# Quarter-array masks, halved values and router products, a merged shift, a re-sorted prologue and regenerated order lists in a two-layer gated model

## The chip, the cores and the metric

The kernel runs on one core of a Trainium2 chip. The metric is the device time of one execution in microseconds (us). Of the kernel before, three runs are shown.

## What is computed

Input x is 8 sequences of 256 tokens of 128 values. Two gated steps follow each other; each adds s * silu(g) to x.

```
xn = layernorm(x)
s  = scan of 32 states over time, y = (c * state) @ Wy + xn @ Wd + biases
g  = two layers of: token shift (upper 64 channels from the token before);
     8-head attention of width 64 in windows of 64 with look-back 64,
     q and k normalised, rotated and scaled; @ wo; residual;
     shift, layernorm, gated GELU MLP of 341; residual
x  = x + s * silu(g)
xn = layernorm(x)
s  = causal attention over 256 tokens, 16 heads of width 8
g  = mixture of 16 experts (SwiGLU 128-256-128, layernorm), two per token
x  = x + s * silu(g)
```

The local attention's mask: with i a query and j a key of its own or the previous window, `(i < j) | (i > j + 64) | (j == -1)` is masked.

## The kernel before, in words

The tokens are 16 tiles of 128 rows. Phase A handles four tiles (two sequences b = 0, 1) in each of four **turns**; phase B ("final") routes tokens and loads experts; phase C runs 48 expert tiles and the output. Phase A is cut into sections: HEAD (the first tiles' norm, q, k, v), FIRST (turn 0), BODY (a hardware loop over turns 1 and 2), TAIL (turn 3) and LAST (the rest of the small attention and the routing). FIRST and BODY also hold the beginning of the next turn; BODY, TAIL and LAST carry the small attention of the turn before (its items begin with b: bqk, bS, bE, bT, bP, bN, bO).

**The order of the work is a computed list.** `PARTS` gives each kind of item its engines and an assumed duration on each; `section_order` runs a list scheduler over them once, at build time, and writes one fixed list per engine. Each engine walks its own list in `run`, in order, and waits on semaphores. So a changed number in `PARTS` changes no arithmetic, and may reorder every engine.

Items that the text speaks of, all for layer l and sequence b: "x" transposes the normalised tiles; "qk" n is one product 128x512 of q or k, then ACT squares it, DVE sums the squares and multiplies by two tables (line 1457), POOL takes the power -0.5 (line 1800) and adds the rotated halves (line 1803), DVE scales (line 1465, item "scale"), PE transposes ("qkT", line 938). "S" is the pair of score banks of one 128-query tile (`scores`), "E" the exponential, "T" the transposes of the probabilities (line 821), "V" the product with the values (`values`), "O" the division, "oT", "wo", then "sh", the shift product, "nh" the layernorm, "hT", three "w1", "w2". "gate" forms the new x, "nm1" and "x1T" norm and transpose it, "router" makes its logits. "ab", "c", "scan", "y" are the state branch.

`scores` opens each of its two banks with one bf16 product, identity (128x128) times a 128x512 mask (line 801), and then adds 16 products of 64 rows by 64 columns each, in four positions of the array (line 812). `values` has, for the first query tile (qt = 0), one product per head with all 128 probability columns as stationary operand, and for qt = 1 two, each with 64 columns. f32 products appear as two records each in the trace, transposes and bf16 products as one.

The prologue: SP issues all loads (x whole, rope tables, first weights, small attention weights, 41 small loads, 2 more, then 12 zero fills of a scratch). POOL makes all constants (identities, shift matrices, masks; lines 1748 to 1775) before anything else. PE and ACT first transpose and copy the five small-attention weights (lines 877, 879), DVE first scales four rope tables (line 1374), and only then does the first tile's norm start (line 1409).

## Time and profile before

| | us |
|---|---|
| median of 3 runs | 936.89 |
| lowest, highest | 935.74, 938.36 |
| the profiled execution's own time | 931.56 |
| its span in the profile | 929.7 |
| PE busy | 727.6 (78%) |
| DVE busy | 635.4 (68%) |
| ACT busy | 506.0 (54%) |
| POOL busy | 391.5 (42%) |

PE is TensorE, DVE VectorE, ACT ScalarE, POOL GpSimd, SP SyncE, which only issues transfers. Times inside the trace count from the span's start. A row of a timeline gives start, length, engine, line, operation, tiles and shape; what stands in brackets is the idle time before it and what ended it. "xN" is a number of instructions. PEclk is the share of the full TensorE clock that was granted.

### The profile page before, as it was taken

The numbers are of one execution on the slowest core, as the hardware profiler recorded it, in microseconds if no ns is written. First come the engines' busy times: TensorE is split into PE (matmuls) and PEld (weight loads), VectorE is DVE, ScalarE is ACT, GpSimd is POOL, SyncE is SP. The second block draws the span as 40 slices with busy tenths as digits, with TensorE's granted clock in tenths as the row PEclk, the third lists the DMA queues.
The fourth block names the chain that finished last, engine by engine and source line by source line (L and its number), as shares of the span: only waits on it lengthen the run. The fifth ranks groups of instructions, "written<-read, shape, count | busy, mean of one in ns | idle before, by whom it ended". The sixth has DMA issues, their size and how long they took to land.

```text
span 929.7 us, 19949 instructions
## 1 busy us (share of the span) xinstructions
PE 727.6 (78%) x6997; PEld 547.7 (59%) x7031; DVE 635.4 (68%) x1521; ACT 506.0 (54%) x901; POOL 391.5 (42%) x470
## 2 busy tenths in 40 slices
PE   2589787599898875898988769885997689698840
PEld 1256465367676753576767447762775567598730
DVE  2586685588779664977796759638676499276645
ACT  1255455365766653756766446543656275487711
POOL 4560651670335034705340545009300437458880
PEclk9799998799999997999999979989999599899975
DMA  5700000000000000000000000000000345212104
GB/s 154 213 1 1 1 1 1 1 1 2 1 2 1 2 1 2 1 2 1 2 1 2 1 2 1 2 1 0 2 2 1 92 135 180 84 59 80 59 38 144
DMA packets 41963, 29.70 MB, mean 32 GB/s; under 512 B 7570, under 2 KB 39308, under 8 KB 41612
## 3 DMA queue, kind: packets, MB, share of 16 engines
q1 hardware_dynamic: 39308, 23.18, 8.6%
q0 software_dynamic: 2560, 5.25, 1.5%
q8 instruction: 60, 0.98, 0.4%
q14 instruction: 35, 0.29, 0.1%
HBM read 18.98 MB, written 9.44 MB: 31 GB/s over the span
## 4 chain that ended last, share of the span: by engine, by line
PE 44%; DVE 20%; POOL 12%; issue 12%; ACT 8%; DMA 1%; SPq 1%; DVEq 0%; POOLq 0%; ACTq 0%
PE psM L782 19%; PE psT L821 4%; ACT arena L1132 4%; PE psO L866 4%; PE psS L851 4%; DVE arena L1457 3%; PE psO L782 3%; PE psS L812 3%; DVE PR L1349 3%; POOL arena L1800 3%; POOL arena L1803 3%; POOL yt_scratch L1826 3%; ACT L1132 2%; POOL RS L1782 2%; DVE arena L1465 2%
## 5 line engine op out<-in xcount | busy, mean ns | idle before, releaser
L782 PE MATMUL psM<-arena 128*128 128x128 f32 (+7 forms) x1168 | 269.3, 374 | 48.0 <-DVE arena L1457 30.3
L1132 ACT ACTIVATE arena<-psT 128x512 f32<-128x512 f32 (+3 forms) x296 | 149.6, 530 | 128.6 <-PE psT L821 44.9
L782 PEld LDWEIGHTS psM<-arena 128*128 128x128 f32 (+5 forms) x1168 | 158.6, 193 | 102.0 <-DVE arena L1457 44.3
L1132 ACT ACTIVATE arena<-psM 128x512 f32<-128x512 f32 (+2 forms) x168 | 88.4, 542 | 126.6 <-PE psM L782 125.7
L1781 POOL TENSOR_SCALAR RS<-MV 128x2 f32<-128x2 f32 x56 | 12.9, 231 | 304.0 <-DVE MV L1490 211.6
L1343 DVE TENSOR_REDUCE MX<-psS 128x4 f32<-128x512 f32 (+1 forms) x160 | 102.7, 683 | 44.9 <-PE psS L851 22.9
L1800 POOL TENSOR_TENSOR arena<-arena,powm 128x8 f32<-128x8 f32 x64 | 109.5, 1711 | 5.3
L1132 ACT ACTIVATE PR<-PR 128x512 f32<-128x512 f32 x160 | 94.9, 626 | 21.0 <-DVE PR L1349 20.7
L1349 DVE TENSOR_TENSOR PR<-psS,MX 128x512 f32<-128x512 f32 x160 | 102.2, 680 | 0.0
L821 PE MATMUL psT<-ident,PR 128*128 128x128 f32 x640 | 91.4, 278 | 10.5 <-ACT PR L1132 6.8
L821 PEld LDWEIGHTS psT<-ident,PR 128*128 128x128 f32 x640 | 71.9, 143 | 34.3 <-issue 22.9
L1803 POOL TENSOR_TENSOR arena<-arena 128x512 f32<-128x512 f32 x64 | 84.1, 1313 | 0.0
L1457 DVE TENSOR_TENSOR arena<-psM,arena 128x512 f32<-128x512 f32 x128 | 81.8, 681 | 3.3 <-POOL arena L1803 3.3
L1132 ACT ACTIVATE arena<-arena 128x768 f32 (+3 forms) x61 | 46.5, 763 | 57.1 <-DVE arena L1722 30.2
L1132 ACT ACT_TABLE_LOAD x51 | 65.4, 1283 | 2.1 <-PEq L1904 1.2
L1799 POOL TENSOR_SCALAR arena<-arena 128x8 f32<-128x8 f32 x64 | 18.2, 284 | 109.9 <-DVE arena L1448 109.3
L1465 DVE TENSOR_TENSOR arena<-arena 128x512 f32<-128x512 f32 x64 | 49.9, 802 | 19.8 <-POOL arena L1803 19.8
L782 PEld LDWEIGHTS psO<-arena,PT 128*64 128x64 f32 (+1 forms) x768 | 48.2, 155 | 14.9 <-issue 11.3
L1448 DVE TENSOR_REDUCE arena<-arena 128x8 f32<-128x512 f32 x64 | 43.5, 679 | 19.5 <-ACT arena L1132 19.1
L851 PE MATMUL psS<-arena 32*128 32x256 f32 (+1 forms) x512 | 55.7, 346 | 0.0
L1826 POOL DMA_INDIRECT yt_scratch<-arena,DEST x48 | 49.9, 1040 | 12.2 <-issue 6.7
L782 PE MATMUL psO<-arena,PT 128*64 128x65 f32 (+1 forms) x768 | 51.5, 241 | 2.9 <-ACT PT L1132 2.9
(196 smaller groups left out, 1142.5 us busy)
## 6 DMA issues: line engine op xcount, KB each, us to landing
arena<-in_L_ffn_w SPq DMA_DIRECT2D x50, 128.0 KB, 2.4
xg_scratch<-zeros SPq DMA_DIRECT2D x12, 256.0 KB, 4.0
arena<-xg_scratch SPq DMA_DIRECT2D x12, 256.0 KB
arena<-yt_scratch SPq DMA_DIRECT2D x4, 512.0 KB, 5.3
arena<-in_L_ffn_wqkv SPq DMA_DIRECT2D x2, 768.0 KB, 5.0
arena<-in_L_ffn_ln_g SPq DMA_DIRECT2D x1, 1024.0 KB, 7.5
arena<-in_L_ffn_ln_b SPq DMA_DIRECT2D x1, 1024.0 KB, 10.4
out<-arena SPq DMA_DIRECT2D x4, 256.0 KB, 2.2
```

The source lines that it names most:

```text
L782: return nc.tensor.matmul(o, lhsT, rhs, start=start, stop=stop)
L821: last = nc.tensor.transpose(bank[:, c * P:(c + 1) * P], PR[:, m % 4, c * P:(c + 1) * P], ident[:])
L851: last = nc.tensor.matmul(Sb[i][:, c * keys:(c + 1) * keys], QL[r, b, lane, qt * P:(qt + 1) * P], KT1[r, b * SEQ:b * SEQ + keys], start=False,
L1132: return nc.scalar.activation(o, i, f, **kw)
L1343: V.tensor_reduce(maxima[i], scores[i], AX, ALU.max).then_inc(dstep, 1)
L1349: V.tensor_tensor(PR[:, (n + i) % 4, :].rearrange("p (s k) -> p s k", s=ns), scores[i], maxima[i].unsqueeze(2).broadcast_to([P, ns, 512 // ...
L1448: V.tensor_reduce(SS[:, m % 4, :], SQ[:, m % 2, :].rearrange("p (h d) -> p h d", h=8), AX, ALU.add).then_inc(ss_done.sem(m), 1)
L1457: last = V.tensor_tensor(dst.rearrange("p (h d) -> p h d", h=8), src, RT[:, 2 * l + n % 2, x, t % 2, :].unsqueeze(1) .broadcast_to([P, 8, ...
L1465: V.tensor_tensor(r1, r1, RN[:, m % 4, :].unsqueeze(2).broadcast_to([P, 8, DH]), ALU.mult)\
L1800: G.tensor_tensor(RN[:, m % 4, :], RN[:, m % 4, :], powm[:, 0:8], ALU.pow)
L1803: G.tensor_tensor(r1, r1, r2[:, :, ::-1, :], ALU.add).then_inc(rope_sum.sem(m), 1)
L1826: G.indirect_dma_start(YT, bass.IndirectOffsetOnAxis(DEST[:, tile:tile + 1], 0), YO[:, tile % OUT_RING, :], None)\
```

## The change

`PARTS`: S on PE 1.8 to 1.5, V 0.9 to 0.6, sh 0.7 to 0.5, router 1.5 to 0.6. All lists are computed anew from them. In `scores` the mask product of a bank becomes two products of 64 rows by 64 columns by 512, so that a pair of banks has four, one in each quarter of the array; two masks with their halves exchanged are made by four transfers from SBUF to SBUF. `values` uses two 64-column products for both query tiles. The shift product of two tiles becomes one of 128 columns. The router's four products become eight of 64 columns. In the prologue x's first four tiles and layer 0's weights come first, 14 loads of the state branch move to ACT's queue, POOL makes only one identity and `powm` first and the rest after the first rstd, layer 0's tables are scaled inside the first "qk", and the small-attention weights are turned after HEAD, through the two O banks.

```diff
-    "S": (("PE", 1.8), ("DVE", 2.4)), "E": (("ACT", 0.58),), "T": (("PE", 0.5), ("ACT", 0.6)),
-    "V": (("PE", 0.9),), "O": (("DVE", 0.7),),
+    "S": (("PE", 1.5), ("DVE", 2.4)), "E": (("ACT", 0.58),), "T": (("PE", 0.5), ("ACT", 0.6)),
+    "V": (("PE", 0.6),), "O": (("DVE", 0.7),),
...
@@ block.sync
-            sp.dma_start(XALL[:], ins["L0_attn_x"].rearrange("b (t p) d -> p (b t) d", p=P)).then_inc(ld_x, 16)
+            sp.dma_start(XALL[:, 0:GT], x_in[:, 0:GT]).then_inc(ld_x0, 16)
+            sp.dma_start(WQKV[:, 0].rearrange("p s n -> p (s n)"), ins["L0_ffn_wqkv"][0]).then_inc(ld_qkv, 16)
...
-            sp.wait_ge(dve_consts, 1)
+            sp.dma_start(XALL[:, GT:NT], x_in[:, GT:NT]).then_inc(ld_x, 16)
...
             sp.wait_ge(pool_consts, POOL_CONSTS)
+            for m, v in zip(swapped, (mask0[0], mask1)):
+                for h in range(2):
+                    sp.dma_start(m[64 * h:64 * h + 64], v[64 - 64 * h:P - 64 * h]).then_inc(ld_masks, 16)
...
@@ scores
                 for i in range(2):
                     pe.wait_ge(s_free.sem(n + i), s_free.reuse(hs, n + i))
-                    nc.tensor.matmul(Sb[i][:], identb[:], (mask0[0], mask1)[qt][:], start=True, stop=False,
-                                     skip_group_check=True)
+                    pe.sem_inc(pe_settled, 1)
+                    r = slice(64 * i, 64 * i + 64)
+                    for w in range(2):
+                        nc.tensor.matmul(Sb[i][64 * w:64 * w + 64, :], identb[r, r],
+                                         ((mask0[0], mask1)[qt] if w == i else swapped[qt])[r, :], start=True, stop=False,
+                                         skip_group_check=True)
@@ values
-                    if qt == 0:
-                        last = mm(bank[:, o], p, VA[:, 2 * b, head, :])
-                    else:
-                        mm(bank[0:64, o], p[:, 0:64], VC[:, b, head, :])
-                        last = mm(bank[64:P, o], p[:, 64:P], VA[:, 2 * b + 1, head, :])
+                    mm(bank[0:64, o], p[:, 0:64], VC[:, b, head, :] if qt else VA[:, 2 * b, head, :])
+                    last = mm(bank[64:P, o], p[:, 64:P], VA[:, 2 * b + qt, head, :])
@@ block.tensor, after HEAD
+            def after_head():
+                pe.wait_ge(ld_raw, 16 * 5)
+                for c in range(4):
+                    last = nc.tensor.transpose(Ob[0][:, c * P:(c + 1) * P], WRAW[:, c, :], ident[:])
+                last.then_inc(raw_turned, 1)
+                nc.tensor.transpose(Ob[1][:, 0:E], WRAW[0:E, 4, :], ident[0:E, 0:E]).then_inc(raw_turned, 1)
+                pe.wait_ge(ld_s5, LOADED_S5)
@@ "sh"
-                        mm(bank[:, 0:64], shift[:], XC[:, 2 * b, 64:D])
-                        mm(bank[:, 64:128], shift[:], XC[:, 2 * b + 1, 64:D], True, False)
-                        mm(bank[:, 64:128], carry[:], XC[:, 2 * b, 64:D], False, True).then_inc(m_full.sem(sec.M[item]), 1)
+                        nc.tensor.matmul(bank[:, 0:128].rearrange("p (t d) -> p t d", t=2), shift[:],
+                                         XC[:, 2 * b:2 * b + 2, 64:D], start=True, stop=False, skip_group_check=True)
+                        nc.tensor.matmul(bank[:, 64:128], carry[:], XC[:, 2 * b, 64:D], start=False, stop=True,
+                                         skip_group_check=True).then_inc(m_full.sem(sec.M[item]), 1)
@@ "router"
-                            last = mm(bank[:, t * E:(t + 1) * E], XN1T[:, t * P:(t + 1) * P], RWT[:])
+                            for h in range(2):
+                                tokens = slice(t * P + 64 * h, t * P + 64 * h + 64)
+                                last = mm(bank[64 * h:64 * h + 64, t * E:(t + 1) * E], XN1T[:, tokens], RWT[:])
@@ block.scalar
+            act.wait_ge(dve_consts, 1)
+            for dst, src in s5_loads:
+                act.dma_start(dst, src).then_inc(ld_s5, 16)
...
             def after_head():
+                act.wait_ge(raw_turned, 2)
+                for i, w in enumerate((WQT, WKT, WVT, WOT)):
+                    act_fn(w[:], Ob[0][:, i * P:(i + 1) * P], ACT.Copy)
+                act_fn(RWT[:], Ob[1][:, 0:E], ACT.Copy).then_inc(raw_kept, 1)
@@ block.vector, first "qk" of HEAD
+                        if sec is HEAD and n == 0:
+                            dve.wait_ge(ld_first, LOADED_FIRST)
+                            scaled_tables(0).then_inc(tables, 1)
+                            dve.wait_ge(tables, 1)
@@ block.gpsimd
+                        if sec is HEAD:
+                            constants()
```

The waits for late loads move to their first use in FIRST: `ld_masks` and `pool_consts` before "S", `raw_kept` before "V", `ld_a` before "wo" and "hT".

**Where instructions move.** First ACT at the very start of the program. Before:

```order
0 L1129 UNCONDITIONAL_BRANCH
1 L1132 ACT_TABLE_LOAD
2 L1132 ACTIVATE WQT<-psT 128x128
3 L1132 ACTIVATE WKT<-psT 128x128
4 L1132 ACTIVATE WVT<-psT 128x128
5 L1132 ACTIVATE WOT<-psT 128x128
6 L1132 ACTIVATE RWT<-psT 128x16
7 L1132 ACTIVATE arena<-psT 128x256
```

And with the change:

```order
7 L1177 DMA arena<-in_L_attn_Wd 128x128
8 L1177 DMA arena<-in_L_attn_Wy 32x128 x2
9 L1177 DMA arena<-in_L_attn_by 128x128
10 L1177 DMA arena<-in_L_attn_bd 128x128
11 L1160 ACT_TABLE_LOAD
12 L1160 ACTIVATE arena<-psT 128x256
13 L1160 ACTIVATE arena<-psT 64x256
```

The 14 transfers now stand ahead of ACT's table load and of its copies for "x"; the five weight copies have moved behind HEAD.

Second, PE in TAIL (the fourth turn), where layer 1's "qk" and "qkT" (line 938, now 955) of the first sequence are issued. L845 (now 857) with L851 (863) is "bS", L821 (836) is "T" or "bT", psM 128x512 is "qk" or "v", L902 (917) is "x". Before:

```order
502 L902 MATMUL psT<-ident,arena 128x128 x2
503 L782 MATMUL psM<-arena 128x512 x3
504 L938 MATMUL psT<-ident,arena 128x128 x4
505 L782 MATMUL psM<-arena 128x512
506 L938 MATMUL psT<-ident,arena 128x128 x4
507 L782 MATMUL psM<-arena 128x512
508 L938 MATMUL psT<-ident,arena 128x128 x4
509 L782 MATMUL psM<-arena 128x512
510 L938 MATMUL psT<-ident,arena 128x128 x4
511 L782 MATMUL psM<-arena 128x512
```

With the change:

```order
545 L917 MATMUL psT<-ident,arena 128x128 x2
546 L793 MATMUL psM<-arena 128x512
547 L836 MATMUL psT<-ident,PR 128x128 x4
548 L793 MATMUL psM<-arena 128x512
549 L955 MATMUL psT<-ident,arena 128x128 x4
550 L857 MATMUL psS<-maskc,identb 128x512 x2
551 L863 MATMUL psS<-arena 128x128 x8
552 L793 MATMUL psM<-arena 128x512
553 L836 MATMUL psT<-ident,PR 128x128 x12
554 L793 MATMUL psM<-arena 128x512 x2
555 L955 MATMUL psT<-ident,arena 128x128 x8
556 L857 MATMUL psS<-maskc,identb 128x2x128 x2
```

Before, nothing of the small attention's second sequence stood among these; now "bqk" of it, three of its six "bS" and six of its twelve "bT" stand ahead of layer 1's "S". In BODY the same happens more mildly. There PE had, in layer 1, the first "S" and at once the "x" of the second sequence:

```order
282 L801 MATMUL psS<-maskl,identb 128x512 x2
283 L812 MATMUL psS<-arena 64x128 x16
284 L899 REGISTER_ALU
285 L902 MATMUL psT<-ident,arena 128x128 x2
286 L782 MATMUL psM<-WOT,arena 128x128 x2
```

and has now:

```order
314 L827 MATMUL psS<-arena 64x128 x16
315 L793 MATMUL psM<-arena 128x128 x6
316 L836 MATMUL psT<-ident,PR 128x128 x4
317 L799 REGISTER_ALU
318 L836 MATMUL psT<-ident,PR 128x128 x4
319 L804 REGISTER_ALU
320 L793 MATMUL psM<-WVT,arena 128x128 x2
321 L793 MATMUL psO<-arena,PT 64x65 x8
322 L833 REGISTER_ALU
323 L836 MATMUL psT<-ident,PR 128x128 x4
324 L857 MATMUL psS<-maskc,identb 128x2x128 x2
325 L863 MATMUL psS<-arena 128x256 x4
```

with the "x" of the second sequence only behind these rows (both "S" of the first sequence stand ahead of them). Of BODY's 172 PE items 107 keep their relative order; HEAD's and LAST's lists are unchanged.

## Rows read from the trace of the kernel before

**Rows 1.** Stretches; busy PE, PEld, DVE, ACT, POOL (instructions), clock, DMA share, GB/s
```profile
0.00:38.30 38.30, 14.62 (x35) 5.96 (x35) 15.66 (x37) 10.09 (x21) 22.92 (x44) 0.98 0.69 188
38.30:185.00 146.70, 112.66 (x908) 79.15 (x914) 98.15 (x228) 70.87 (x126) 60.82 (x66) 0.92 0.04 10
...
367.10:546.60 179.50, 153.68 (x1560) 113.08 (x1568) 133.80 (x288) 107.83 (x186) 67.48 (x74) 0.97 0.01 2
546.60:724.00 177.40, 149.05 (x1529) 111.93 (x1536) 121.39 (x267) 100.34 (x171) 53.45 (x60) 0.94 0.01 1
...
804.00:929.70 125.70, 77.42 (x628) 73.53 (x628) 72.72 (x263) 65.55 (x125) 73.12 (x96) 0.84 0.24 76
```

**Rows 2.** Timeline of the prologue: start us, length us, engine, line, tiles
```profile
1.20 1.28 ACT L1132 ACT_TABLE_LOAD   x1 [1.20 <-PEq L1904]
...
1.85 0.27 DVE L1366 MEMSET arena<- 128x256 f32 x1 [1.85 <-issue]
...
9.26 0.41 POOL L1775 TENSOR_SCALAR_AFFINE_SELECT maskl<-maskl 64x256 bf16<-64x256 bf16 x1
...
10.16 0.42 SPq L734 DMA_DIRECT2D arena<-in_L_attn_Wa  x1
...
11.71 1.43 DVE L1374 TENSOR_TENSOR arena<-arena 128x256 f32<-128x256 f32 x4 [9.24 <-DMA arena<-in_L_ffn_k_scale]
...
13.18 0.49 DVE L1409 BATCH_NORM_STATS2 ST<-XALL 128x6 f32<-128x128 f32 x2
...
16.95 1.03 ACT L1132 ACTIVATE arena<-psT 128x256 f32<-128x256 f32 x3 [2.21 <-PE psT L902]
...
18.03 3.78 PE L782 MATMUL psM<-arena 128*128 128x512 f32 x4 [1.19 <-ACT arena L1132]
...
21.66 0.25 POOL L1799 TENSOR_SCALAR arena<-arena 128x8 f32<-128x8 f32 x1 [6.37 <-DVE arena L1448]
...
30.49 9.96 SPq L740 DMA_DIRECT2D xg_scratch<-zeros  x12
...
34.38 1.26 POOL L1803 TENSOR_TENSOR arena<-arena 128x512 f32<-128x512 f32 x1
```

**Rows 3.** DMA issues of the first 14 us: KB each, us to landing
```profile
XALL<-in_L_attn_x SPq DMA_DIRECT2D x1, 0.5 KB, 6.6
```

**Rows 4.** Timeline of PE: masks, values, router beside what follows each
```profile
274.01 0.59 PE L801 MATMUL psS<-maskl,identb 128*128 128x512 bf16 x2
274.53 1.10 PE L812 MATMUL psS<-arena 64*64 64x128 f32 x32
...
282.88 1.90 PE L782 MATMUL psO<-arena,PT 128*128 128x65 f32 x16
284.61 1.08 PE L782 MATMUL psM<-arena 128*128 128x512 f32 x2
...
387.36 0.69 PE L782 MATMUL psO<-arena,PT 128*64 128x65 f32 x16
387.97 0.66 PE L961 MATMUL psT<-ident,arena 128*128 128x128 f32 x4
...
544.47 1.89 PE L782 MATMUL psM<-RWT,arena 128*128 128x16 f32 x8 [0.55 <-ACT arena L1132]
```

**Rows 5.** Groups of PE by shape, whole run: busy us, mean ns, idle before
```profile
L782 PE MATMUL psM<-arena,shift 128*128 128x64 f32 x64 | 9.5, 271 | 0.0
```

**Rows 6.** Chain of waits, fourth turn: shares by line
```profile
by line: PE psM L782 23.6%; issue 7.9%; PE psT L821 7.1%; PE psO L866 6.3%; PE psS L851 6.1%; PE psO L782 5.9%; POOL arena L1800 5.9%; POOL arena L1803 5.2%; DVE PR L1349 4.1%; PE psS L812 4.0%; ACT arena L1132 3.9%; PE psT L961 2.3%; ACT L
```

**Rows 7.** Two stretches of the fourth turn, columns as in rows 1
```profile
631.00:655.00 24.00, 15.28 (x79) 7.88 (x80) 17.24 (x28) 10.84 (x20) 22.97 (x21) 0.93 0.00 0
655.00:715.00 60.00, 54.61 (x673) 44.11 (x675) 42.48 (x101) 40.99 (x67) 6.87 (x12) 1.00 0.01 2
```

**Rows 8.** The page, groups of DVE: busy us, mean ns, idle before
```profile
L1343 DVE TENSOR_REDUCE MX<-psS 128x4 f32<-128x512 f32 (+1 forms) x160 | 102.7, 683 | 44.9 <-PE psS L851 22.9
...
L1349 DVE TENSOR_TENSOR PR<-psS,MX 128x512 f32<-128x512 f32 x160 | 102.2, 680 | 0.0
```

More of the change, by code:

```diff
@@ L106 @@
     "gate": (("ACT", 0.42), ("DVE", 1.9), ("Pool", 1.0)), "nm1": (("DVE", 0.6),),
-    "x1T": (("PE", 0.3), ("ACT", 0.4), ("Pool", 0.4)), "router": (("PE", 1.5), ("DVE", 0.3)),
+    "x1T": (("PE", 0.3), ("ACT", 0.4), ("Pool", 0.4)), "router": (("PE", 0.6), ("DVE", 0.3)),
     "bqk": (("PE", 1.9), ("ACT", 0.75)), "bqm": (("Pool", 0.95),), "bv": (("PE", 0.5), ("DVE", 0.42)),
@@ L474, in gated_layers @@
         mask1 = sb("maskl1", [P, 512], BF16)
+        swapped = [sb(f"swapped{k}", [P, 512], BF16) for k in range(2)]
         shift = sb("shift", [P, P])
@@ L927, in run @@
                         t, i = (n // 2, n % 2) if kind == "qk" else (n, 2)
+                        if sec is HEAD and item == ("qk", 0, 0):
+                            pe.wait_ge(ld_qkv, 16)
                         if kind == "qk" and n % 4 == 0:
@@ L942, in run @@
                         l, b, qt = of
+                        if sec is FIRST:
+                            pe.wait_ge(ld_masks, 16 * 4)
+                        if sec is FIRST and (l, b, qt) == (0, 0, 0):
+                            pe.wait_ge(pool_consts, POOL_CONSTS)
                         if qt == 0:
@@ L952, in run @@
                         l, b, k = of
+                        if sec is FIRST:
+                            pe.wait_ge(raw_kept, 1)
                         values(b, k, ht, sec.T["T", l, b, k], ho, sec.O[item], sec.AU[*of])
@@ L965, in run @@
                         l, b = of
+                        if sec is FIRST:
+                            pe.wait_ge(ld_a, LOADED_A)
                         copied(("oT", l, 2 * b), ("oT", l, 2 * b + 1))
@@ L1219, in run @@
                         l, b = of
+                        if sec is FIRST:
+                            act.wait_ge(ld_a, LOADED_A)
                         bank, free = from_t(item)
@@ L1475, in run @@
                         l, b = of
+                        if sec is FIRST:
+                            dve.wait_ge(ld_a, LOADED_A)
+                            dve.wait_ge(ld_l1, 16 * 2)
                         bank, free = m_bank(item)
@@ L1744, in step @@
                 pool.wait_ge(pstep, steps[0] + steps[1])
-            for v, c in ((ident, 0.0), (identb, 0.0), (shift, 0.0), (carry, 0.0), (trib, 1.0), (onesb, 1.0),
-                         (powm, -0.5), (zeros, 0.0), (headm, 1.0), (mask0[0], 0.0), (mask1, 0.0), (mask0[1], 0.0)):
-                G.memset(v[:], c).then_inc(pool_consts, 1)
-            pool.wait_ge(pool_consts, 12)
             one = dict(compare_op=ALU.not_equal, fill=1.0, channel_multiplier=1)
-            for v, base in ((ident, 0), (identb, 0), (shift, 1), (carry, -(P - 1))):
-                G.affine_select(out=v[:], in_=v[:], base=base, pattern=[[-1, P]], **one).then_inc(pool_consts, 1)
```

119 lines of the change are left out of this document (60 added, 59 removed), and 2 rows, old and new, of the table PARTS.

## The prediction

> **What bounds the kernel now.** I read the stretches first [rows 1]. Three of the shown ones belong to phase A: the prologue, 38.3 us, with PE busy only 14.6; turn 0, 146.7; and turns 2 and 3 of 179.5 and 177.4 (turn 1, not shown, is the same loop body as turn 2). In the turns PE is the busiest engine, 153.7 of 179.5 us in turn 2, and DVE next with 133.8. So PE bounds much of a turn but not all: 26 us of turn 2 and 28 of turn 3 have no matmul. The experts' stretch of 125.7 us and the routing before it are untouched: their lists are the same. Second, the timeline of the prologue [rows 2]: DVE waits until 11.71 us for the first loads, starts the first tile's statistics at 13.18, ACT copies the turned tile at 16.95, PE starts the first q at 18.03, and then POOL works through four "qk" from 21.66 to 35.64, 14.0 us, with hardly a gap. POOL sets that end. Third, PE's timeline around the operations that change [rows 4] and the shift group [rows 5]. Fourth, the chain of waits of turn 3 [rows 6]: its PE lines alone (products, transposes, scores) make about 55%, POOL's two 11%. Last, two stretches of turn 3 [rows 7]: from 631 to 655 POOL is busy 23.0 of 24 us and PE 15.3 (eight "qk" of layer 1 pass through POOL), and right after it, from 655 to 715, PE is busy 54.6 of 60. One is starved of matmuls, the next is full of them.
>
> **The prologue.** A quarter of x now stands alone at the front. The whole x landed 6.6 us after its issue [rows 3]; a quarter lies between 2 and 6.6, and I take 3.5 (most of the 6.6 was bytes), so DVE starts at about 4.4. From there to ACT's copies took 3.8 us (13.18 to 16.95), which would give 8.2. But ACT now issues 14 transfers first. SP spent 20.33 us on 43 of them (10.16 to 30.49), 0.473 each; 14 are 6.6 us, from the end of DVE's first memset at 2.1, so to 8.7, and the 1.28 us table load stands behind them in the order: 10.0. The copies start at 10.0 and not 16.95, **7.0 earlier**. Two others come close to that time. POOL's constants, done at 9.67 before, now follow the first rstd (about 6.5, between the statistics at 4.4 and the copies at 8.2 at the earliest) with, as an estimate, 8 of their 9.67 us, so to 14.5, while the first "qk" reaches POOL at 21.66 - 7.0 = 14.7. The scaling of layer 0's tables, half of the 1.43 us in the row, goes into the first "qk" on DVE and is hidden under POOL's power. POOL's 14.0 us are unchanged. Behind HEAD PE turns five weights, at 0.66 per four [rows 4] some 0.7, ahead of the first scores. Net **6.3**. Bounds: 8.0 if ACT does not bind (8.75 less 0.7), 3 if POOL or the layer 0 weights come late. The other late loads are covered: SP has 30 transfers between 10.2 and the masks (14.2 us, to 24.4), four masks take 1.9, and with a landing of at most 6.6 they are there at 32.9, against first scores at 32. That is 1 us in the worst case and nothing at a usual landing. If POOL were late, SP and DVE too would wait for its constants.
>
> **The four PE edits**, each by the time from its start to the start of what follows [rows 4].
> - Masks: a pair took 274.01 to 274.53, 0.52. Of that 0.31 lies between the second mask and the first score product. The scores, in the same four quarters, run four at a time. If the masks do too, the four take as long as one, 0.21 and a little; I take a saving of 0.28. Bounds: 0.3, and a loss of 0.4 if the four run in turn. 32 pairs, 8 a turn.
> - Values: two full ones take 282.88 to 284.61, 0.87 each; one in halves 387.36 to 387.97, 0.61. Saving 0.25, 8 a turn.
> - Shift: 64 records take 9.5 us [rows 5], 0.59 per item for four; two of twice the columns about 0.4. Saving 0.2, 4 a turn; bounds 0 and 0.3.
> - Router: 1.89 us for eight records at the turn's end; sixteen with halves, by the ratio of the values (0.61 to 0.87), 1.33. Saving 0.55, once a turn; bounds: a loss of 1.9 if a product costs the same whatever its size, a gain of 1.3.
>
> A turn saves 2.2 + 2.0 + 0.8 + 0.55 = 5.6 us of PE, four turns 22. The added counter increment of PE ahead of each mask has no row; it is between 0 and 0.1 (the layout change, the smallest gap in the rows), and I take 0, because the wait it carries stood there before. What of the 22 shortens the run is the share in which PE is the chain, 55% [rows 6]: **12**. Bounds 0 and 22. The rest falls where PE waits for POOL or DVE.
>
> The masks' rows show a change of array layout at 0.1 us: 0.31 before the first score product against 0.21 between masks. The values' 0.61 includes entering and leaving it. The Trainium skill ("TensorEngine Tiling (Array Packing)", Key Properties) says that changing the tiling mode drains the engine, which speaks against halving the values between full-size transposes: it adds two changes to each of 32 values, and saves one at each pair of scores. By 0.1 us for each, were it not in the 0.61 already, the sum would be 3 us worse. The same page (Instruction Overhead) gives each matmul some 60 cycles whatever its size, and by that the router's sixteen records of 16 columns would cost twice the eight, the loss of 1.9 named above; against it stand the half-size values, 16 records in 0.61 us and 8 full ones in 0.87.
>
> **The new lists.** In turn 3 three "bS" (each two mask products and eight row products), six "bT" and a "bqk" move from behind 655 us into the stretch in which PE waits for POOL. By their neighbours a "bT" is about 0.5 (four transposes 0.66 from start to end [rows 4], overlapping what follows), and a "bS" and a "bqk" about 1.5 and 1.9, estimated from the scores' 0.52 for masks and about 1 for products; they are 3 x 1.5 + 6 x 0.5 + 1.9 = 9.4 us of PE. From the full stretch 9.4 go, and the other one had 8.7 us to spare [rows 7]. I take **8**. Bounds: 12, and nothing if it ends POOL's rhythm (below). In BODY the first sequence's second scores, its "T", "V" and one more "bS" move ahead of the second "x" in the same way; there is less idle time in one piece, and the turn's end (gate, norm, transpose, router, one after another) stays. I take 3 a turn, **6** for two, bounds -8 and 16. FIRST keeps 112 of 126 items in order: nothing, within 2.
>
> **Sum.** 6.3 + 12 + 8 + 6 = 32.3 us off the profiled execution's 931.56: 899.3. The median of the runs is 5.3 above that execution, so the prediction for the median is 904.6.
>
> **Rivals.**
> 1. *The lists give nothing.* A list in fixed order is only as good as its 50 or so other durations, which are unchanged. For it: DVE is busy 133.8 of 179.5 in turn 2, and filling PE's gaps fills DVE's too. Against: turn 3's two stretches. Then 18.3 remain: 918.6.
> 2. *The lists give more*, as PE, freed by 22 us, leaves DVE and ACT room: both 22 in full and twice the gain of the lists, 6.3 + 22 + 28 = 56: 881.
> 3. *The packing doesn't happen*: the mask quarters run in turn, and the router pays per product. That is 32 x 0.4 + 4 x 1.9 = 20 us more PE where the sum counts 11 saved (9.0 and 2.2), 31 apart, 55% of it 17: 922. This is also where the tiling page's overhead rule leads. Against it stand the score products, 32 records of 128 columns in 1.10 us [rows 4], 0.034 each where a full one takes 0.1.
> 4. *Slower: the pulled-in items break POOL's rhythm.* POOL needs a fresh "qk" from DVE every 3.5 us (14.0 / 4), and each "bS" puts 2 x (0.683 + 0.680) = 2.7 us of DVE [rows 8] ahead of one. Three of them in turn 3 delay POOL by 8. In BODY the second sequence's "x", and with it its four "qk" (14 us of POOL), starts behind some eight more PE items, some 8 us with their waits. If what was pulled in is then missed later instead of saved, 8 + 2 x 8 = 24 us are lost against 18.3 gained: 942. The point from which it decides is 6 us lost per turn in three turns. Against it: the total of each engine's work in a turn falls or stays, and what was pulled in needn't be done later.
>
> **How the numbers follow.** Chances: forecast 0.55, rival 1 0.18, rival 2 0.10, rival 3 0.07, rival 4 0.06; the rest, 0.04, is something small in all (a late load in the prologue, a list that only loses a little) at about 935. The likeliest gives 904.6; its own range by the bounds is 893 to 916. The range for 8 in 10 takes in rival 1 and part of 2 and 3: 886 to 923. A change of less than 0.3% (2.8 us) can't be told from none here. Faster needs 934.1 or less: 0.91; within: 0.03; slower: 0.06.
>
> **What would show it.** The first q product at about 11 us instead of 18.03; POOL's first power near 15 and the first scores near 32. Mask records of 64 by 64 starting close together, with the first score product 0.25 to 0.3 after the first mask; values of both tiles at 0.6. PE busy 22 us less in all. Turn 3 at about 166, turns 1 and 2 at about 173 to 176, turn 0 near 143; in turn 3 PE busy above 18 of 24 us while POOL works through layer 1's "qk". Wrong would be: a prologue still above 34, a pair of masks above 0.5 us, or a turn longer than before with POOL idle between two "qk" of one sequence.

## The result: no faster, 0.46% slower

| | before | changed |
|---|---|---|
| median of 20 runs each, us | 935.6 | 938.62 |
| lowest, highest | 929.22, 938.68 | 936.5, 941.24 |
| profiled execution: own time, span | 931.56, 929.7 | 939.3, 937.0 |
| PE busy | 727.6 | 726.5 |

The ratio is 1.0046, 95% interval 1.0032 to 1.0061. The forecast was 904.6 with a range of 886 to 923. The page of the changed kernel, its first lines:

```profile
span 937.0 us, 20709 instructions
...
PE 726.5 (78%) x7337; PEld 541.1 (58%) x7351; DVE 633.2 (68%) x1521; ACT 504.9 (54%) x900; POOL 396.8 (42%) x470
...
PEclk9899997799999877899998978999999599999985
```

PE's busy time has hardly moved although the forecast took 22 us out of it, and the granted clock is lower: 0.90 in turn 2 below, 0.96 before by the same cut. The four turns, as stretches (columns as in [rows 1]; each line is one turn):

```profile
32.38:178.72 146.34, 114.24 (x997) 78.17 (x1000) 98.22 (x228) 71.19 (x131) 61.56 (x66) 0.90 0.06 15
178.72:370.31 191.59, 157.54 (x1644) 114.63 (x1648) 132.59 (x289) 110.54 (x188) 68.64 (x74) 0.91 0.01 2
370.31:564.90 194.59, 157.46 (x1648) 114.71 (x1656) 132.60 (x288) 110.83 (x188) 68.63 (x74) 0.90 0.01 2
564.90:730.27 165.37, 140.11 (x1615) 103.02 (x1612) 121.84 (x266) 93.84 (x166) 55.59 (x60) 0.96 0.01 1
```

Turn 0 is 146.3 (before 146.7), turns 1 and 2 are 191.6 and 194.6, turn 3 is 165.4 (before 177.4). From here on every turn is cut at the moment when DVE writes the router's logits; by that cut the four turns of the kernel before are 146.5, 179.8, 181.8 and 177.3. The stretch to the first scores fell from 38.4 to 32.4, and what follows turn 3 is 206.7 (before 205.9). So the changed kernel is 6 us ahead when turn 0 starts, gains another 12 in turn 3, and loses 12 to 13 in each of the two turns of BODY. These are two single executions, 7.7 us apart; the medians are 3.0 apart.

**What came as forecast.** The prologue, in the timeline:

```profile
3.91 0.49 DVE L1438 BATCH_NORM_STATS2 ST<-XALL 128x6 f32<-128x128 f32 x2 [1.45 <-DMA XALL<-in_L_attn_x]
...
6.07 2.45 DVE L1393 TENSOR_SCALAR arena<-XALL,MV,RS 128x128 f32<-128x128 f32 x2 [1.28 <-POOL RS L1823]
...
8.35 0.46 ACTq L1177 DMA_DIRECT2D arena<-in_L_attn_bd  x1
...
8.78 0.66 PE L917 MATMUL psT<-ident,arena 128*128 128x128 f32 x2 [8.78 <-DVE arena L1393]
...
9.52 1.28 ACT L1160 ACT_TABLE_LOAD   x1 [9.52 <-PE psT L917]
...
10.81 1.04 ACT L1160 ACTIVATE arena<-psT 128x256 f32<-128x256 f32 x3
...
11.95 3.75 PE L793 MATMUL psM<-arena 128*128 128x512 f32 x4 [2.52 <-issue]
...
15.53 0.25 POOL L1843 TENSOR_SCALAR arena<-arena 128x8 f32<-128x8 f32 x1 [1.68 <-DVE arena L1477]
```

The statistics start at 3.91, ACT's last of 14 transfers is issued at 8.35, the copies stand at 10.81 and the first q at 11.95 (forecast 11; before 18.03). POOL starts the first "qk" at 15.53 (before 21.66). One thing is different in it: the copies wait for the transposes at 8.78, since the norm of two tiles took 2.45 us on DVE from 6.07, while POOL was writing its constants. ACT's transfers ended at 8.81, and its table load then waited until 9.52 for the transposes, so the norm was the later of the two.

The masks, in PE's timeline of a layer 1 "S" in turn 2:

```profile
468.25 0.40 PE L815 MATMUL psS<-maskl,identb 64*64 64x512 bf16 x1
468.25 0.40 PE L815 MATMUL psS<-swapped,identb 64*64 64x512 bf16 x2
468.26 0.40 PE L815 MATMUL psS<-maskl,identb 64*64 64x512 bf16 x1
468.49 1.04 PE L827 MATMUL psS<-arena 64*64 64x128 f32 x32
```

The four quarters start within 0.01 us, and the first score product 0.24 after them; before it was 0.52 [rows 4]. And the router at the end of turn 2, with the masks of the next turn behind it:

```profile
563.70 1.04 PE L793 MATMUL psM<-RWT,arena 128*64 128x16 f32 x16 [0.47 <-ACT arena L1160]
564.67 0.63 PE L815 MATMUL psS<-maskl,identb 64*64 64x512 bf16 x1
```

From its start to the next start are 0.97 us, 2.11 before (544.47 to the next row of PE at 546.58): a saving of 1.1 where I had taken 0.55. Both stand at a granted clock of 0.50, the lower of its two levels. In e12 below, where the whole products have the quartered masks behind them, the same distance is 1.82 (543.24 to 545.06): 0.85 is the router's own, the rest goes with the mask product that follows.

Turn 3's starved stretch, which [rows 7] shows with 15.28 us of PE in 24:

```profile
645.00:669.00 24.00, 17.96 (x91) 9.84 (x92) 23.10 (x37) 15.07 (x29) 21.54 (x20) 1.00 0.00 0
```

PE now fits 17.96 us of matmuls in while POOL is busy 21.54 (forecast: above 18).

### The profile page after: what moved, and what is told of

Its sections match the earlier page's. It is cut to its first block, busy times and chain, and to the rows that moved or that the text cites. A ratio compares the mean times of both kernels' runs of the same rounds, so it can differ in the third digit from the quotient of the medians.

```text
span 937.0 us, 20709 instructions
## 1 busy us (share of the span) xinstructions
PE 726.5 (78%) x7337; PEld 541.1 (58%) x7351; DVE 633.2 (68%) x1521; ACT 504.9 (54%) x900; POOL 396.8 (42%) x470
## 3 DMA queue, kind: packets, MB, share of 16 engines
q0 software_dynamic: 2560, 5.25, 1.5%
## 4 chain that ended last, share of the span: by engine, by line
PE 45%; DVE 22%; issue 12%; POOL 10%; ACT 9%; DMA 1%; DVEq 0%; ACTq 0%; POOLq 0%; SPq 0%
PE psM L793 19%; ACT arena L1160 5%; DVE arena L1490 5%; PE psT L836 4%; PE psO L878 4%; PE psS L863 4%; PE psS L827 3%; POOL yt_scratch L1870 3%; PE psO L793 3%; DVE PR L1378 3%; POOL RS L1823 2%; DVE arena L1477 2%; ACT L1160 2%; DVE arena L1498 1%; POOL arena L1847 1%
## 5 line engine op out<-in xcount | busy, mean ns | idle before, releaser
L793 PE MATMUL psM<-arena 128*128 128x128 f32 (+7 forms) x1168 | 279.2, 384 | 51.9 <-DVE arena L1490 22.6
L793 PEld LDWEIGHTS psM<-arena 128*128 128x128 f32 (+5 forms) x1168 | 162.1, 195 | 111.2 <-DVE arena L1490 39.5
L1160 ACT ACTIVATE arena<-psT 128x512 f32<-128x512 f32 (+2 forms) x296 | 150.4, 530 | 127.0 <-PE psT L955 29.2
L836 PE MATMUL psT<-ident,PR 128*128 128x128 f32 x640 | 95.0, 282 | 10.5 <-ACT PR L1160 8.2
L836 PEld LDWEIGHTS psT<-ident,PR 128*128 128x128 f32 x640 | 75.1, 146 | 37.9 <-issue 20.7
L1843 POOL TENSOR_SCALAR arena<-arena 128x8 f32<-128x8 f32 x64 | 21.1, 330 | 148.9 <-DVE arena L1477 148.9
L1160 ACT ACT_TABLE_LOAD x50 | 64.2, 1283 | 10.4 <-PE psT L917 9.5
L1498 DVE TENSOR_TENSOR arena<-arena 128x512 f32<-128x512 f32 x64 | 47.2, 751 | 18.0 <-POOL arena L1847 17.9
L1160 ACT ACTIVATE PT<-psT 128x512 f32<-128x512 f32 x64 | 36.6, 596 | 35.0 <-PE psT L836 23.1
L1858 POOL TENSOR_SCALAR arena<-arena,lanem 128x256 f32<-128x256 f32 x32 | 29.3, 931 | 60.0 <-ACT arena L1160 60.0
```

Source lines behind the costliest of these rows:

```text
L793: return nc.tensor.matmul(o, lhsT, rhs, start=start, stop=stop)
L836: last = nc.tensor.transpose(bank[:, c * P:(c + 1) * P], PR[:, m % 4, c * P:(c + 1) * P], ident[:])
L1160: return nc.scalar.activation(o, i, f, **kw)
L1498: V.tensor_tensor(r1, r1, RN[:, m % 4, :].unsqueeze(2).broadcast_to([P, 8, DH]), ALU.mult)\
```

## Experiments

All were timed in five rounds beside the kernel before; its median in the four groups was 935.32, 933.64, 933.57 and 933.12, and is given as "before" where it matters. "L" in an expectation means the first theory, "M" its rival.

**The first four** take the change apart: which list, or which product, costs? The first three put other durations into `section_order`:

```diff
     after = section_items(head, rest, attn, final)
-    length = {(i, e): duration(i, e) for i in after for e, _ in PARTS[i[0]]}
+    other = {"S": 1.8, "V": 0.9, "sh": 0.7, "router": 1.5} if COND else {}
+    length = {(i, e): other.get(i[0], duration(i, e)) if e == "PE" else duration(i, e)
+              for i in after for e, _ in PARTS[i[0]]}
```

e1_edits_old_lists: COND is True, so all lists are those of before.

> The whole change, but every section's lists computed with the durations of before (S 1.8, V 0.9, sh 0.7, router 1.5 on PE), so PE, ACT, DVE and POOL have exactly the lists of before. Theory L (the new list of BODY costs 12 us in each of turns 1 and 2, the four PE edits are worth little): the kernel before minus 6 for the prologue and minus 0 to 8 for the edits, so 0.985 to 0.994 of before. Rival M (the packed masks or halved values themselves cost time in BODY, whatever the list): turns 1 and 2 stay above 185 us each and the run is at 1.00 of before or above.

Measured 916.39, ratio 0.9808 (0.9781 to 0.9835). The edits and the prologue are worth 18.9 us, more than either theory allowed: L had 0 to 8 for the edits.

e2_lists_only: the kernel before, with the reverse (the change's four durations in every section).

> The kernel before with nothing but the new lists (prologue, masks, values, shift and router as before). Theory L: turns 1 and 2 longer by 10 to 14 us each, turn 3 shorter by 5 to 10, together 10 to 20 us slower, 1.011 to 1.021 of before. Rival M: within 3 us of before in turns 1 and 2.

Measured 952.9, ratio 1.0202 (1.0174 to 1.0231). Turns: 147.4, 192.1, 194.6, 169.2. The lists alone cost 17.6 us, and BODY's turns are as long as in the changed kernel, without any of its edits.

e3_old_list_body: the changed kernel, COND is `head and attn`, which is BODY alone.

> The whole change, but BODY alone has the lists of before; FIRST and TAIL keep the new ones. Theory L: turn 3 stays at 165 us, turns 1 and 2 go back to 175 to 182, the run is 18 to 30 us faster than before (0.968 to 0.981). Rival M: turns 1 and 2 stay at 190 and the run is at 1.00.

Measured 912.06, ratio 0.9742 (0.9709 to 0.9775). Its three later turns:

```profile
180.14:358.26 178.12, 151.35 (x1644) 109.33 (x1648) 133.65 (x289) 107.93 (x186) 67.81 (x74) 0.95 0.01 2
358.26:537.76 179.50, 150.74 (x1648) 109.99 (x1656) 132.63 (x288) 107.88 (x186) 67.81 (x74) 0.95 0.01 2
537.76:703.76 166.00, 140.62 (x1615) 102.96 (x1614) 122.05 (x266) 93.98 (x166) 55.52 (x60) 0.96 0.01 2
```

Same instructions, same counts, only the order of one section differs: turns 1 and 2 are 13.5 and 15.1 us shorter. PE is busy 150.74 us in turn 2 and not 157.46, at a granted clock of 0.95 instead of 0.90.

e4_whole_masks: the changed kernel with the mask product of before in `scores`.

```diff
-                    r = slice(64 * i, 64 * i + 64)
-                    for w in range(2):
-                        nc.tensor.matmul(Sb[i][64 * w:64 * w + 64, :], identb[r, r],
...
+                    nc.tensor.matmul(Sb[i][:], identb[:], (mask0[0], mask1)[qt][:], start=True, stop=False,
+                                     skip_group_check=True)
```

> The whole change with its new lists, but the mask of a score bank is again one product of the full array. Theory L: within 3 us of the changed kernel, since the masks are not what costs. Rival M: 6 to 15 us faster than the changed kernel, mostly in turns 1 and 2.

Measured 944.92, ratio 1.0125 (1.0088 to 1.0161): quartered masks are worth 6.3 us (7.4 by the ratios), more than L's 3, and M has the wrong sign. So BODY's list is the whole loss, and the rival "the packed forms cost" is out.

**Where in BODY?** I followed each item of turn 2 on DVE, where no record is missing. Up to 70 us after the turn's start there is little between the two (POOL's fifth "qk" starts at 70.1 in the changed kernel, at 68.8 in e3). Then comes the first layer's MLP of the second sequence. DVE's multiplications of its three "w1" and the addition of "w2" in the changed kernel (the turn begins at 370.31):

```profile
453.12 0.47 DVE L1540 SCALAR_TENSOR_TENSOR arena<-psM,arena 128x256 f32<-128x256 f32 x1
...
463.27 0.47 DVE L1540 SCALAR_TENSOR_TENSOR arena<-psM,arena 128x256 f32<-128x256 f32 x1
...
471.99 0.47 DVE L1540 SCALAR_TENSOR_TENSOR arena<-psM,arena 85x256 f32<-85x256 f32 x1
...
475.92 0.41 DVE L1547 TENSOR_TENSOR arena<-arena,psM 128x256 f32<-128x256 f32 x1
```

and in e3 (begins at 358.26):

```profile
440.43 0.48 DVE L1542 SCALAR_TENSOR_TENSOR arena<-psM,arena 128x256 f32<-128x256 f32 x1
...
443.19 0.48 DVE L1542 SCALAR_TENSOR_TENSOR arena<-psM,arena 128x256 f32<-128x256 f32 x1
445.99 0.48 DVE L1542 SCALAR_TENSOR_TENSOR arena<-psM,arena 85x256 f32<-85x256 f32 x1 [2.31 <-ACT arena L1162]
...
450.23 0.41 DVE L1549 TENSOR_TENSOR arena<-arena,psM 128x256 f32<-128x256 f32 x1
```

82.8, 93.0, 101.7 and 105.6 us after the turn's start, against 82.2, 84.9, 87.7 and 92.0. ACT in the same piece of the changed kernel; 256 columns (128 or 85 rows) are a gelu, PR is an exponential:

```profile
451.07 0.48 ACT L1160 ACTIVATE arena<-psM,arena 128x256 f32<-128x256 f32 x1
451.56 1.28 ACT L1160 ACT_TABLE_LOAD   x1
452.86 1.15 ACT L1160 ACTIVATE PR<-PR 128x512 f32<-128x512 f32 x2
...
460.05 1.28 ACT L1160 ACT_TABLE_LOAD   x1
461.34 0.47 ACT L1160 ACTIVATE arena<-psM,arena 128x256 f32<-128x256 f32 x1
...
462.32 1.28 ACT L1160 ACT_TABLE_LOAD   x1
463.62 1.15 ACT L1160 ACTIVATE PR<-PR 128x512 f32<-128x512 f32 x2
...
469.37 1.28 ACT L1160 ACT_TABLE_LOAD   x1
470.67 0.47 ACT L1160 ACTIVATE arena<-psM,arena 85x256 f32<-85x256 f32 x1
```

and in e3:

```profile
437.46 1.15 ACT L1162 ACTIVATE PR<-PR 128x512 f32<-128x512 f32 x2
438.63 1.28 ACT L1162 ACT_TABLE_LOAD   x1
439.92 0.48 ACT L1162 ACTIVATE arena<-psM,arena 128x256 f32<-128x256 f32 x1
442.42 0.48 ACT L1162 ACTIVATE arena<-psM,arena 128x256 f32<-128x256 f32 x1 [2.03 <-PE psM L795]
...
445.48 0.47 ACT L1162 ACTIVATE arena<-psM,arena 85x256 f32<-85x256 f32 x1
...
451.43 1.28 ACT L1162 ACT_TABLE_LOAD   x1
452.73 0.63 ACT L1162 ACTIVATE PR<-PR 128x512 f32<-128x512 f32 x1
```

In e3 the two exponentials of bS(1,0,0) are done (437.46) before the first gelu, and the three gelus share one table load. In the changed kernel each gelu has its own, with exponentials between them. Its list has bS(1,0,0) right behind the first "w1", where the list of before has it right ahead, and bS(1,0,1) ahead of the third "w1", where it was behind. Between the first gelu and the second ACT spends 2.6 us on two table loads, 1.15 on exponentials and 3.5 on copies, and waits 2.5. In the whole turn there are 16 table loads against 14. PE's waits for the "w1" multiplication in turn 2:

```profile
PE psM L793 <- DVE arena L1540: 5.9, 3, 3.1
PE psM L793 <- DVE arena L1490: 5.2, 6, 1.3
PE psT L1036 <- DVE arena L1393: 4.8, 1, 4.8
```

e3 has no such row among its longest (what stands there is 3.9 us for line 1492, which is line 1490 here, and 3.2 for the norm). Everything behind "w2" is then late: POOL's second group of layer 1's "qk" starts 113.3 us into the turn and not at 98.9. Of these 14.4 us "w2" is already 13.6 late, and the turn as a whole is 15.1 longer, so nearly the whole loss of the changed kernel is made in this piece.

I did not have this reading at once. First I held the late "x" itself for the cause. The next runs add one rule to the planner, for BODY only (the list up to the held item stays the changed one):

```diff
             parts = [(i, e)]
+    for item, held in [(("bS", 1, 0, 1), (("x", 1, 1), "PE"))] if head and attn else ():
+        before[item, "PE"] = before[item, "PE"] + [held]
```

e5_bo_late, with the pair (bO(1), w2(1,1)):

> The changed kernel with one item of BODY's list moved: bO(1) goes behind w2(1,1), as in the list before. In the changed kernel's trace PE stands 2.67 us at bO(1) (532.35) until DVE has done its bN, with the second sequence's hT, w1 and the next turn's first x queued behind. Theory X (the 13 to 15 us per BODY turn are mostly the second layer 1 'x' coming 14 us late, the end of the turn adds about 4 by its own order): 1 to 2.5 us per turn, 2 to 5 in all, about 935. Rival Y (the loss is made at the end of the turn, by bO's wait and by what it holds): 5 or more per turn, 10 or more in all, below 929.

Measured 941.7, ratio 1.0097 (1.0071 to 1.0123): nothing won. The wait of 2.67 us went, and PE waits 3.57 at "hT" (536.21) for DVE's norm instead: it was no loss on the path.

e6_end_as_before, with (bO(1), w2(1,1)) and (x(0,0), w1(1,1,1)):

> As e5, and the next turn's x(0,0) with its first two 'qk' also stands behind w1(1,1,1), as in the list before; the other items of BODY keep the order of the changed kernel. Before, the four 'qk' of the next turn started on POOL 3.2, 3.2 and 3.7 us apart; in the changed kernel 6.7, 3.9 and 3.7. Theory X: these 4 us per turn come back, with what e5 brings 4 to 6 per turn, 8 to 12 in all, about 929. Rival Y: the whole loss sits here, 13 per turn, about 912.

Measured 937.73, ratio 1.0049 (1.0026 to 1.0072), BODY 191.6 and 194.6 as in the changed kernel, in an execution 6.5 us above its median. The four "qk" did come 3.2, 3.1 and 3.7 apart, but the first of them 5 us later. Both predictions failed: the 4 us were not there to be had.

e7_bs_behind_x, the diff above:

> The changed kernel with one rule for BODY: bS(1,0,1) may not start on PE before x(1,1). The list up to that item is the changed kernel's, and behind it S, x(1,1) and its 'qk' come as early as in the list before; bO(1) still stands ahead of hT(1,1). Theory X: the second group of layer 1's 'qk' starts on POOL about 99 to 102 us after the turn's start instead of 113, and the turn is 8 to 11 us shorter, 16 to 22 in all: 917 to 923. Rival Y (the place of x is harmless, as POOL has 47 idle us around it): within 4 us of the changed kernel, 935 to 939.

Measured 934.32, ratio 1.001 (0.9992 to 1.0028). The group of "qk" came at 106.4 instead of 113.3, and the turns fell by 3.4 and 3.8 only. X had promised 8 to 11 and an earlier "x" (Y, within 4 us of the changed kernel, missed by 0.3); its own trace told why: the second "w1" was still multiplied at 92.4, since bS(1,0,0) still stood in front of it.

e8_only_tail_list, COND is `head`:

> All the edits of the change, FIRST and BODY with the lists before (computed from 1.8, 0.9, 0.7 and 1.5), TAIL alone with the new one. It differs from e3 (912.06, there) by FIRST's list only, where 14 of 126 PE items move. If that list is worth nothing: 912, within 1.5. If it gives something, e1's turn 0 of 146.8 against e3's 148.3 says that it costs 1 to 1.5: about 910.5. Theory X and Rival Y say the same here.

Measured 907.67, ratio 0.9731 (0.971 to 0.9752), below the 910.5 to 912 expected. Against e1 (0.9808) TAIL's list is worth 7.2 us. Against e3 (0.9742) FIRST's list costs something between 1 (by the ratios) and 3 us (by the medians less "before"); the intervals overlap.

e9_bs_behind_w1, with the pair (bS(1,0,0), w1(0,1,2)):

> The changed kernel with one rule for BODY, earlier in the list than e7's: bS(1,0,0) may not start on PE before w1(0,1,2). In the changed list it stands between w1(0,1,0) and w1(0,1,1), and ACT has its two exponentials, and then those of bS(1,0,1), between the three gelus. On the chip DVE multiplied these three w1 at 82.8, 93.0 and 101.7 us after the turn's start, in e3 at 82.2, 84.9 and 87.7; w2(0,1) followed at 105.6 against 92.0. Theory Z (this split of the first layer's MLP is where BODY loses): w1 at about 80, 83 and 86, layer 1's second group of 'qk' before 102, a turn about as in e3, 177 to 180, so 911 to 915 in all. The planner's own clock gives BODY 186.7 with this rule, 194.1 without and 187.7 for the list before. Rival W (e7 won 7 us at the second 'x' and the turn fell by 4 only, so the loss is made later, around wo(1,1) and sh(1,1)): 930 or more.

Measured 925.76, ratio 0.9936 (0.9912 to 0.9959): between the two. The "w1" stood at 81.5, 84.3 and 86.9 and "w2" at 89.3 as Z said, and the group of "qk" at 98.0. But the turns were 184.4 and 187.7, and the run is between Z's range and W's. What is left is not a second half of the changed kernel's loss: behind the held item the planner orders everything anew, and the new end of the turn costs. e9's timeline of PE, at the end of turn 2 (line 1013 is "hT" of the second sequence, line 880 bP(1,1), line 919 "x", psM 128x256 "w1"):

```profile
513.90 0.66 PE L1013 MATMUL psT<-ident,arena 128*128 128x128 f32 x2
514.66 5.25 PE L880 MATMUL psO<-arena 128*32 128x128 f32 x128
519.84 1.13 PE L795 MATMUL psM<-arena 128*128 128x256 f32 x4
...
525.11 3.47 PE L795 MATMUL psM<-arena 128*128 128x512 f32 x6 [2.84 <-DVE arena L1542]
```

The small attention's last product, 128 records and 5.25 us, stands between "hT" and the first "w1" of the turn's last MLP, and ACT loads the gelu table only behind it (522.77). The first "w1" is multiplied at 162.2, in e3 at 154.5. In the changed kernel's list, as in that of before, bP(1,1) stands ahead of "hT" (524.85 in turn 2); its first "w1" there comes at 169.4, 14.9 after e3's, which is about the 14 us from further up.

e13_bp_behind_w1, e9's pair and (bP(1,1), w1(1,1,2)):

> e9 (925.76, there) with a second rule: bP(1,1) may not start on PE before w1(1,1,2). In e9's trace it stands right behind hT(1,1), takes 5.25 us (514.66) and pushes the second sequence's last MLP back: nh at 147 to 149 us of the turn as in e3 (145 to 147), but the first w1 multiplied at 162.2 against 154.5. Theory Z2 (the list's other half of the loss is the small attention's last product in the way of the turn's last MLP): w1 at 155 to 157, 5 to 7 us less per turn, so 912 to 916. The planner's clock gives BODY 184.5 against 186.7, by which it would be 4.4 in all, 921. Rival V (the end is bound by something else, as moving bO alone in e5 gave nothing): 924 or more.

Measured 913.36, ratio 0.979 (0.9765 to 0.9815), turns 1 and 2 of 174.5 and 180.8. Two rules bring 25.3 of the 26.5 us back that lie between the changed kernel and e3. The first "w1" of the last MLP came at 158.6, and Z2's 155 to 157 holds all the same: this list puts two "qkT" behind the router, so turn 2 is counted from some 3 us earlier (the first "w1" further up stands at 84.6, in e9 at 81.5), and turn 3 holds more (171.2, in e9 168.1). Less these 3.1 it is 155.5. The medians fell by 12.4, 6.2 per turn, where the planner's clock gave 4.4 in all.

**The planner's own clock.** `section_order` keeps a finish time for every item, from its durations, the bank limits and the table loads. Its last finish time is the section's length on its clock. For the first two rows the list was held fixed and timed with the change's durations; on the chip a turn of BODY is the mean of turns 1 and 2 of one profiled execution.

| list | FIRST clock, chip | BODY clock, chip | TAIL clock, chip |
|---|---|---|---|
| of before, with the edits (e1) | 155.2, 146.8 | 187.7, 179.0 | 184.6, 172.4 |
| of the change | 156.3, 146.3 | 194.1, 193.1 | 176.0, 165.4 |
| e7 | | 195.8, 189.5 | |
| e9 | | 186.7, 186.1 | |
| e13 | | 184.5, 177.7 | |
| e10, searched | 148.8, 145.5 | 177.3, 173.2 | 162.3, 158.5 |
| e14, second of the search | 149.1, 143.4 | 178.1, 177.3 | 163.1, 158.9 |

e13's 177.7 is too short by 1 to 2, as its turn 3 holds what the cut took from BODY. With shorter durations for four kinds the greedy planner ends BODY later (194.1 against 187.7 for the list it replaced) and TAIL earlier. The chip agrees with both signs. It even has the three "w1" at 82.1, 92.1 and 100.5, against 82.8, 93.0 and 101.7 on the chip.

Lists that lie close it does not rank. e7's list is 1.7 longer than the change's on the clock and 3.6 shorter on the chip. e9's is 1.0 shorter than the list of before and 7.1 longer on the chip. For FIRST the traces can't tell: in the eight kernels that have all edits and the changed FIRST list turn 0 took 145.9 to 151.9. (BODY's mean is steadier: with the list of before and all edits it is 179.0 in e1, 178.8 in e3 and 178.4 in e8.)

So I let it choose:

```diff
-    length = {(i, e): duration(i, e) for i in after for e, _ in PARTS[i[0]]}
+    seed, spread = {(True, True, False, False): (1384, 0.1), (True, True, True, False): (529, 0.25),
+                    (False, True, True, False): (868, 0.1)}.get((head, rest, attn, final), (0, 0))
+    draw = random.Random(seed)
+    factor = {(k, e): round(1 + draw.uniform(-spread, spread), 3) for k, v in PARTS.items() for e, _ in v}
+    length = {(i, e): duration(i, e) * factor[i[0], e] for i in after for e, _ in PARTS[i[0]]}
```

e10_lists_searched:

> All edits of the change; the durations that FIRST, BODY and TAIL are planned from are each multiplied by a drawn factor (0.9 to 1.1, 0.75 to 1.25, 0.9 to 1.1), and of 4400 lists per section that one is taken which ends first on the planner's clock with the change's durations unaltered. That clock gives FIRST 148.8 (156.3 as changed, 155.2 as before), BODY 177.3 (194.1, 187.7), TAIL 162.3 (176.0, 184.6). If the clock tells lists apart on the chip as it seems to have for the two known ones: 7 + 2 x 15 + 11 = 48 us below the changed kernel, 890, or 880 if it understates as it did for BODY (6.4 on the clock, 13 to 15 on the chip). If a list so chosen only fits the planner's model and not the chip: about 905 to 938.

(The list taken is the one with the lowest mean over the change's durations and six variants of them, each factor within 12%; the clock's figures are with the durations unaltered.)

Measured **887.86**, ratio 0.9506 (0.948 to 0.9531): faster than both kernels, by 5% and, against the changed kernel's 938.62, by 5.4%. Turns 1 to 3:

```profile
177.44:349.50 172.06, 151.81 (x1648) 110.99 (x1652) 133.27 (x288) 105.36 (x184) 68.86 (x74) 0.95 0.01 2
349.50:523.84 174.34, 151.77 (x1648) 111.08 (x1656) 133.09 (x288) 104.92 (x183) 68.80 (x74) 0.94 0.01 2
523.84:682.34 158.50, 141.54 (x1614) 106.25 (x1612) 122.81 (x267) 96.72 (x168) 52.38 (x60) 0.96 0.01 2
```

e11_body_searched, only BODY's entry of the table:

> As e10, but only BODY has the searched list; FIRST and TAIL are the changed kernel's. If the planner's clock holds on the chip: BODY 10 us shorter than with the list before (177.3 against 187.7), so 912.06 (e3) less 2 x 10 = 892. If the searched list only fits the model: between 905 and 938.

Measured 900.66, ratio 0.965 (0.9634 to 0.9665). The turns are 171.9 and 175.0. That is between the two outcomes expected. Against e3 it won 11 us and not 20: e3's list runs 9 us faster on the chip than on the planner's clock, the searched one 4.

e14_lists_second:

> As e10 (887.86, there), with the list that ended second on the planner's clock in each section: FIRST 149.1, BODY 178.1, TAIL 163.1 (e10's 148.8, 177.3, 162.3). If the clock ranks lists on the chip, and e10 was no lucky draw: 3 us above e10, 891, and not outside 883 to 900. If e10 was luck: above 900.

Measured 890.83, ratio 0.9543 (0.9517 to 0.9569), 3.0 us above e10 as said. So e10 was no single lucky draw, but the 3 us themselves are luck: BODY is 4.1 a turn longer where the clock has 0.8, and turn 0 2.1 shorter where it has 0.3 longer.

**The size of the PE edits.** e12_values_router_old, e8 with the values of the first query tile and the router as before:

```diff
-                    mm(bank[0:64, o], p[:, 0:64], VC[:, b, head, :] if qt else VA[:, 2 * b, head, :])
-                    last = mm(bank[64:P, o], p[:, 64:P], VA[:, 2 * b + qt, head, :])
+                    if qt == 0:
+                        last = mm(bank[:, o], p, VA[:, 2 * b, head, :])
...
-                                last = mm(bank[64 * h:64 * h + 64, t * E:(t + 1) * E], XN1T[:, tokens], RWT[:])
+                            last = mm(bank[:, t * E:(t + 1) * E], XN1T[:, t * P:(t + 1) * P], RWT[:])
```

> The kernel of e8 (907.67, there) with two of the four edits of PE taken back: the values of the first query tile with 128 probability columns again, and the router's four whole products. All lists are e8's. The prediction priced them at 2.0 and 0.55 us of PE a turn and 55% of that on the path: 5.6 us in all, so 913. If changing the array's layout twice more per item costs what the halves save: 907 to 909. If PE bounds these turns in full: 10, so 918.

Measured 915.63, ratio 0.9814 (0.9795 to 0.9832): the two edits are worth 8.0 us, between the 5.6 priced and the 10 of "PE bounds these turns in full".

## Why the prediction was wrong

- **Prologue**, forecast 6.3: right. 38.4 to 32.4 is 6.0. The copies came at 10.8, not 10.0, and behind the slow norm, which the sum carried at its old length of 0.60, and not behind the transfers.
- **Four PE edits**, forecast 12: right in size, partly by luck. e1's 18.9 less the prologue's 6.0 leaves 12.9. By parts: masks 6.3 (forecast 8.8 of PE, 55% of it 4.8), values with router 8.0 (5.6); the shift was not taken back by itself, and the difference leaves it nothing. The prices were too low: a pair of masks saves 0.28 as forecast, but a value 0.33 and not 0.25, and the router 0.85 to 1.1 and not 0.55, so that these two save 14 to 15 us of PE and not 10.2. The 8.0 are 55% of that. With the masks' 9.0 and the shift's 3.4 (15.7 us busy before, 12.3 now) PE was saved 26 to 28 us and not 22, and the share on the path was about half and not 55%.
- They brought nothing in **turn 0** (forecast 143, measured 146.3, with the old list 146.8). With e1 POOL starts its second four "qk" 54.3, 57.5, 60.8 and 64.2 us into the turn, before 54.3, 57.5, 60.8 and 64.2. PE did not become idle in their place: it is busy 116.4 us at a granted clock of 0.87 in e1's turn 0 and 112.7 at 0.92 before. That POOL sets the pace of this turn fits, but no run tries it.
- **TAIL's list**, forecast 8: right, 7.2 (e8 against e1). Turn 3 was forecast at 166 and took 165.4.
- **BODY's lists**, "I take 3 a turn, 6 for two, bounds -8 and 16": this step failed. The term took what was moved ahead as saved, as in TAIL. BODY's lists cost 26.5 us (938.62 against e3's 912.06), over 3 times the bound. All the rest of the sum held: 6.0 + 12.9 + 7.2 = 26.1 gained, 26.5 lost there, 1 to 3 in FIRST.
- Rival 4 had the sign, the place (BODY's second "x" with its "qk", which came 14 us late) and almost the time (942). It had 0.06, its mechanism was mostly wrong, and its number came near by two errors that offset: it lost 8 in TAIL, where the same reordering gained 7, and 16 in BODY, where 26.5 were lost. I priced eight more PE items ahead of "x", but from "w2" to that "qk" are 7.7 us, in e3 6.9. What made it late lies before "w2", in the first layer's MLP: bS(1,0,0) moved from ahead of the three "w1" to between them, bS(1,0,1) from behind them, and ACT, PE and DVE took up the exponentials, copies and gelus in that order. e9 shows the place: with bS(1,0,0) held behind the three "w1", "w2" came at 89.3 and the "qk" at 98.0. That ACT's table loads are the reason is read from the trace and not tried alone. From the first gelu to the third are four loads, 5.1 us, and none in e3; the other 9 of the 14 us are waits in order and other work between.
- The argument against rival 4, "what was pulled in needn't be done later", is the error behind the number. Moving work is only free if it stands in front of nothing that others wait for, on any of the four engines. I had looked at PE's list and never at ACT's around the same items. e9 shows it once more: its list lost again at the turn's end, by a bP(1,1) between "hT" and the last MLP, where neither the changed kernel nor the one before has it, and e13 took that back.
- The values' two added layout changes, which the Trainium skill ("TensorEngine Tiling (Array Packing)", Key Properties) speaks against, cost nothing net: e12, without them and with the whole router, is 8.0 slower. The loss that the prediction named by the page's overhead per matmul (Instruction Overhead) did not come: the router's 32 records took 7.5 us busy, 64 of half the columns 4.2.

## What to carry to other kernels

When an order is computed by a greedy planner, a better duration for one item does not make a better list: read the finish time that the planner gives the new list and that of the old list under the new durations, section by section. It needs no run. Here it had the right sign where the two were 6 us or more apart (BODY, TAIL, the searched lists) and the wrong one for e7 against the changed list (1.7) and for e9 against the old list (1.0); e13's 3.2 against the old list brought nothing. A close call still needs the chip. Choosing among many drawn lists by it gave 3% on top of the 2% of the prologue and all edits. In the list itself look at the engine with switched modes: an item of another kind between items of one kind costs two switches (here 1.28 us each), and all that waits in order behind them.
